# One ScalarE read of PSUM per quarter, differences and copies a slot later, extra banks and shorter routing in a two-layer expert and recurrence kernel

## What is computed

```python
x = x + 0.5 * ffn(layernorm(x))
x = x + attn(layernorm(x))
x = x + 0.5 * ffn(layernorm(x))

def ffn(x):                                   # 8 experts, 512 hidden channels, the best 2 of 8 count
    probs = softmax(x @ router_w.T)
    top_w, top_idx = top_k(probs, 2);  top_w = top_w / (sum(top_w) + 1e-9)
    y = relu(x @ w1[e].T + b1[e]) @ w2[e].T + b2[e]          # for every e
    return sum over the two chosen e of top_w * y
def attn(x):                                  # a gated linear recurrence over time, 4 heads, 16 keys, 32 values
    S = exp(w_t) * S + k_t v_t ;  o_t = q_t (S + u k_t v_t)
    o = groupnorm(o) * gn_weight + gn_bias;  return (o * silu(g)) @ W_o.T
```

## Time and profile before

| | |
|---|---|
| median of 3 runs | 491.46 us |
| the profiled execution's own time | 491.48 us |
| its span, first to last instruction | 489.6 us |
| TensorE busy | 477.3 us, 97% |
| VectorE busy | 367.5 us, 75% |
| ScalarE busy | 338.0 us, 69% |
| GpSimd busy | 240.8 us, 49% |
| TensorE's granted clock | 1.00 over the whole span |

### The profile page before, as it was taken

One profiled execution on the slowest core, in us unless ns is written; L12 is line 12 of the kernel. 1 busy time (PEld: TensorE's weight loads), 2 busy tenths in 40 slices (PEclk: granted clock), 3 DMA queues, 4 the chain that ended last, 5 costly groups with the idle time before them and its releaser, 6 DMA issues.

```text
span 489.6 us, 6291 instructions
## 1 busy us (share of the span) xinstructions
PE 477.3 (97%) x1873; PEld 302.0 (62%) x1873; DVE 367.5 (75%) x714; ACT 338.0 (69%) x569; POOL 240.8 (49%) x252
## 2 busy tenths in 40 slices
PE   8999999999999999999999999999999999999996
PEld 4676776566557556555755755565566565777775
DVE  3889877759975895997496799935669994667644
ACT  3776787677757668773857767646778765687874
POOL 3235632627875162886516268834616874321322
PEclk9999999999999999999999999999999999999999
DMA  7771121058410017730003555111046611003200
GB/s 252 233 269 33 54 64 41 7 154 234 129 43 1 1 44 208 204 106 1 1 2 129 150 175 151 44 64 43 1 120 182 195 43 44 0 1 117 79 1 21
DMA packets 21297, 44.59 MB, mean 91 GB/s; under 512 B 3856, under 2 KB 4240, under 8 KB 21264
## 3 DMA queue, kind: packets, MB, share of 16 engines
q1 hardware_dynamic: 14928, 32.66, 21.5%
q10 hardware_dynamic: 6336, 11.54, 8.3%
HBM read 40.91 MB, written 3.28 MB: 90 GB/s over the span
## 4 chain that ended last, share of the span: by engine, by line
PE 58%; issue 16%; POOL 11%; DVE 10%; ACT 3%; DMA 1%; POOLq 0%; ACTq 0%; DVEq 0%
PE Y L377 12%; PE U L346 8%; PE U L350 7%; PE U L347 7%; POOL qs L955 5%; PE Y L368 4%; PE Y L373 4%; PE Y L370 4%; POOL xT L929 4%; DVE hid_lo L773 2%; PE A L450 2%; PE A L442 1%; POOL pool_a L961 1%; PE A L436 1%; DVE gy L782 1%
## 5 line engine op out<-in xcount | busy, mean ns | idle before, releaser
L929 POOL TENSOR_TENSOR xT<-xT,gy 128x512 f32<-128x512 f32 x63 | 84.3, 1338 | 146.2 <-DVE gy L782 146.0
L346 PE MATMUL U<-xhi,w1lo 128*128 128x512 f32 x256 | 151.6, 592 | 3.0 <-ACT hid_hi L575 1.2
L377 PE MATMUL Y<-hid,w 128*128 128x512 f32 x264 | 134.2, 589 | 0.0
L773 DVE TENSOR_TENSOR hid_lo<-hid,hid_hi 128x512 fp32r<-128x512 f32 x124 | 97.8, 793 | 39.0 <-ACT hid_hi L575 38.5
L577 ACT ACTIVATE hid<-U,small 128x512 f32<-128x512 f32 x132 | 90.6, 689 | 48.6 <-PE U L350 46.2
L574 ACT ACTIVATE hid<-U,small 128x512 f32<-128x512 f32 x124 | 85.5, 690 | 43.8 <-PE U L350 39.3
L350 PE MATMUL U<-xlo,w1hi 128*128 128x512 f32 x256 | 100.8, 394 | 0.0
L347 PE MATMUL U<-xhi,w1hi 128*128 128x512 f32 x256 | 100.5, 392 | 0.0
L955 POOL TENSOR_TENSOR qs<-q,pool_a 128x512 f32<-128x512 f32 x64 | 80.1, 1251 | 15.0 <-DVE pool_a L830 14.8
L346 PEld LDWEIGHTS U<-xhi,w1lo 128*128 128x128 f32 x256 | 48.1, 188 | 62.1 <-issue 35.9
L575 ACT ACTIVATE hid_hi<-U,small 128x512 fp32r<-128x512 f32 x124 | 84.8, 684 | 0.0
(11 more groups left out here) (135 smaller groups left out, 515.9 us busy)
## 6 DMA issues: line engine op xcount, KB each, us to landing
G<-gate_dram SPq DMA_DIRECT2D x32, 512.0 KB, 4.3
vb<-v_dram ACTq DMA_DIRECT2D x44, 256.0 KB, 3.6
vb<-v_dram SPq DMA_DIRECT2D x20, 256.0 KB, 4.5
pool_a<-wexp_dram SPq DMA_DIRECT2D x8, 256.0 KB, 6.8
w<-wexp_dram SPq DMA_DIRECT2D x8, 256.0 KB, 6.8
v_dram<-v SPq DMA_DIRECT2D x8, 256.0 KB, 2.2
xnt<-xtok_dram SPq DMA_DIRECT2D x4, 256.0 KB, 5.1
xT<-xT_dram SPq DMA_DIRECT2D x4, 256.0 KB, 7.1
```

What stands on the lines that cost most here:

```text
L346: mm(dst, w1lo[:, e, f, :], xhi[:, k % NB, :], start=True, stop=False)
L377: last = mm(dst, w2[:, g % E, f, :], hid[:, n % HS, cut], start=first, stop=final)
L773: dve.tensor_tensor(hid_lo[:, c, :], hid[:, n % HS, :], hid_hi[:, c, :], ALU.subtract).then_inc(h_lo, 1)
L929: pool.tensor_tensor(xT[:, h, b, :], xT[:, h, b, :], gy[:, g % 2, :], ALU.add).then_inc(acc, 1)
```

## The change

1. ScalarE reads PSUM once a quarter. `h_f` is counted after that one instruction. The upper part is copied from `hid` in SBUF by a new `upper(n - 1)` that stands behind `relu(n)`, a slot later, with a semaphore of its own (`h_hi`).
2. VectorE's difference of quarter n is made in slot n+2 instead of n+1. TensorE still takes it in slot n+3.
3. Parts: quarters 112, 144 and 192 lose them, twelve fourth quarters (51, 83, 123, 167, 171, 215, 219, 235, 239, 243, 247, 251) gain them. For these VectorE makes the upper part too (a cast, then the difference), and all three down matmuls wait for it. In all 133 quarters in parts. `PS` goes from 3 to 4 buffers. GpSimd splits the fourth quarters of w2 in slots 33 to 41.
4. w1's upper parts of experts 2 to 7 are made on GpSimd, ahead of w2's, instead of on VectorE.
5. Experts 2 and 3 sum in banks A1 and A2, which are free in the first block, and the first two combines move to slots 13 and 14.
6. Routing works on the exponentials before they are normalised: 17 linked small instructions a block instead of 20, in 9 steps, which for block 1 are spread over 9 slots instead of 5.

```diff
+ROUTE = 9
-FP, PS, GS, VS = 3, 3, 6, 5
+FP, PS, GS, VS = 3, 4, 6, 5
+def route_slots(k):
+    return {1: 9, 2: 5, 3: 5}.get(k, 3)
 def route_steps(k, t):
+    return [1 + n for n in range(ROUTE) if n * route_slots(k) // ROUTE == t]
-    return 4 * g + {0: 10}.get(g, 7)
-LATE = (slot_of(2, T_PO) + 1, slot_of(2, T_PO) + 5)
+    return 4 * g + {0: 13, 1: 10}.get(g, 7)
+LATE = (112, 144, 164, 168, 192)
+LAST_PARTS = (33, 37, 39, 41)
+QUIET = (51, 83, 123, 167, 171, 215, 219, 235, 239, 243, 247, 251)
+def by_vector(n):
+    return n % FC == FP and n in QUIET
...
-    return n >= FC and n % FC < (1 if scans else FP) and n not in LATE
+    return n >= FC and n % FC < (1 if scans else FP) and n not in LATE or by_vector(n)
...
+        def rows_of(g):
+            return A[g - 1] if g in (2, 3) else Y[g % 2]
...
-                if f == 0 and g >= 2:
-                    pe.wait_ge(comb, g - 1)
+                if f == 0 and g >= 4:
+                    pe.wait_ge(comb, g - 1 if g >= 6 else g - 3)
...
+                    if not by_vector(n):
+                        pe.wait_ge(h_hi, uppers_to(n + 1))
+                    if f == FP:
+                        pe.wait_ge(w2lo_s, E + g % E // 2 + 1)
+                        pe.wait_ge(h_lo, parts_to(n + 1))
...
-                    act.activation(hid[:, n % HS, :], U[n % 2][:, :], ACT.Relu, bias=bias)
-                    act.activation(hid_hi[:, c % PS, :], U[n % 2][:, :], ACT.Relu, bias=bias).then_inc(h_f, 1)
+                act.activation(hid[:, n % HS, :], U[n % 2][:, :], ACT.Relu, bias=w(W_B1 + n % (E * FC), 1)).then_inc(h_f, 1)
+            def upper(n):
+                if n >= 0 and in_parts(n) and not by_vector(n):
...
+                    act.activation(hid_hi[:, c % PS, :], hid[:, n % HS, :], ACT.Copy).then_inc(h_hi, 1)
...
                 relu(n)
+                upper(n - 1)
...
-                    dve.wait_ge(h_f, n + 1)
+                    if not by_vector(n):
+                        dve.wait_ge(h_hi, uppers_to(n + 1))
+                    else:
+                        dve.wait_ge(h_f, n + 1)
+                        dve.wait_ge(down, PARTS[PARTS.index(n) - PS] + 1)
+                        link(dve.tensor_copy(hid_hi[:, c, :], hid[:, n % HS, :]))
...
-                if n >= 1:
-                    split_h(n - 1)
+                if n >= 2:
+                    split_h(n - 2)
...
+            def w1_upper(e):
+                pool.wait_ge(w1_in[e], 16)
+                if e == 2:
+                    pool.wait_ge(w1hi_s, 2)
+                pool.tensor_copy(w1hi[:, e].rearrange("p f n -> p (f n)"), w1raw[:, e, :]).then_inc(w1hi_s, 1)
...
+                if n % 4 == 0 and n // 4 + 2 < E:
+                    w1_upper(n // 4 + 2)
```

More of the change, by code:

```diff
@@ L117, in combine_slot, with uppers_to @@
 def combine_slot(g):
-    return 4 * g + {0: 10}.get(g, 7)
-LATE = (slot_of(2, T_PO) + 1, slot_of(2, T_PO) + 5)
+    return 4 * g + {0: 13, 1: 10}.get(g, 7)
[4 more added lines that the diff above has]
+    return n % FC == FP and n in QUIET
 def in_parts(n):
     scans = any(slot_of(i, T_SC) - 3 <= n < slot_of(i, T_PO if i == UNITS - 1 else T_OUT) for i in range(UNITS))
-    return n >= FC and n % FC < (1 if scans else FP) and n not in LATE
+    return n >= FC and n % FC < (1 if scans else FP) and n not in LATE or by_vector(n)
 def parts_to(n):
     return sum(in_parts(k) for k in range(n))
+def uppers_to(n):
+    return sum(in_parts(k) and not by_vector(k) for k in range(n))
 PARTS = [n for n in range(ALL) if in_parts(n)]
@@ L170, in program @@
         gate_T = sb("gate_T", [P, NB, 32])
-        w2hi = sb("w2hi", [P, E, FP, P], F32R)
-        w2lo = sb("w2lo", [P, E, FP, P], F32R)
+        w2hi = sb("w2hi", [P, E, FC, P], F32R)
+        w2lo = sb("w2lo", [P, E, FC, P], F32R)
         G = sb("G", [P, GS, NT])
@@ L220, in program @@
         half_s, hv_r, hr_r, hx_r, hr_p = (sem(n) for n in ("half_s", "hv_r", "hr_r", "hx_r", "hr_p"))
-        up, h_f, h_lo, down = sem("up"), sem("h_f"), sem("h_lo"), sem("down")
+        up, h_f, h_hi, h_lo, down = sem("up"), sem("h_f"), sem("h_hi"), sem("h_lo"), sem("down")
         w2hi_s, w2lo_s = sem("w2hi_s"), sem("w2lo_s")
@@ L738, in route @@
                 if step == 1:
+                    dve.wait_ge(lg_sub, k + 1)
+                    link(dve.scalar_tensor_tensor(out=flat(m(3)), in0=flat(m(0)), scalar=0.0, in1=flat(tie4),
+                                                  op0=ALU.is_equal, op1=ALU.mult))
+                    link(dve.tensor_reduce(r(5), m(3), AX.X, ALU.max))
+                if step == 2:
+                    link(dve.tensor_tensor(m(4), tie4, bc(r(5)), ALU.is_equal))
+                    link(dve.scalar_tensor_tensor(out=flat(m(6)), in0=flat(m(4)), scalar=-1e30, in1=flat(m(0)),
+                                                  op0=ALU.mult, op1=ALU.add))
@@ new lines, in route @@
+                if step == 3:
+                    link(dve.tensor_reduce(r(4), m(6), AX.X, ALU.max))
+                    link(dve.tensor_tensor(m(3), m(6), bc(r(4)), ALU.is_equal))
+                if step == 4:
+                    link(dve.tensor_tensor(m(3), m(3), tie4, ALU.mult))
+                    link(dve.tensor_reduce(r(5), m(3), AX.X, ALU.max))
+                if step == 5:
+                    link(dve.tensor_tensor(m(5), tie4, bc(r(5)), ALU.is_equal))
+                    link(dve.tensor_tensor(m(7), m(4), m(5), ALU.add))
@@ L749, in route @@
[L749 to L759 removed]
+                    link(dve.tensor_tensor(m(3), m(7), m(1), ALU.mult))
@@ L760, in route @@
+                if step == 7:
+                    link(dve.tensor_reduce(r(3), m(3), AX.X, ALU.add))
+                    link(dve.scalar_tensor_tensor(out=r(6), in0=r(1), scalar=1e-9, in1=r(3), op0=ALU.mult, op1=ALU.add))
+                if step == 8:
+                    link(dve.reciprocal(r(7), r(6)))
+                if step == 9:
+                    link(dve.scalar_tensor_tensor(out=gate[:, b].rearrange("p e t -> p t e"), in0=m(3), scalar=0.5, in1=bc(r(7)),
                                                   op0=ALU.mult, op1=ALU.mult))
-                if step == 5:
-                    link(dve.scalar_tensor_tensor(out=r(6), in0=r(3), scalar=1e-9, in1=r(4), op0=ALU.add, op1=ALU.add))
-                    link(dve.reciprocal(r(7), r(6)))
-                    link(dve.tensor_tensor(gate[:, b].rearrange("p e t -> p t e"), m(3), bc(r(7)), ALU.mult))
@@ L781, in combine @@
                     dve.wait_ge(acc, g - 1)
-                dve.scalar_tensor_tensor(out=gy[:, g % 2, :], in0=Y[g % 2][:, :], scalar=w(W_B2 + e, 1),
+                dve.scalar_tensor_tensor(out=gy[:, g % 2, :], in0=rows_of(g)[:, :], scalar=w(W_B2 + e, 1),
                                          in1=G[:, g % GS, :], op0=ALU.add, op1=ALU.mult).then_inc(comb, 1)
@@ L915, in _ @@
                     attend(i, step_of(i, n))
+            split_h(ALL - 2)
             split_h(ALL - 1)
@@ L1075 @@
     arrays = lay_out(inputs)
-    nc = bacc.Bacc("TRN2", target_bir_lowering=False, num_devices=1)
+    nc = bacc.Bacc("TRN2", target_bir_lowering=False, num_devices=1, dynamic_dma_scratch_size=1024)
     args = [nc.dram_tensor(n, a.shape, F32, kind="ExternalInput").ap() for n, a in arrays.items()]
```

48 lines of the change are left out of this document (16 added, 32 removed).

## The result

The changed kernel takes **502.1 us** (median of 4 runs, 501.08 to 502.86), the kernel before 491.38 beside it: a ratio of 1.0218, 95% interval 1.0206 to 1.0231. Forecast was 486.4, range 482.8 to 489.6. It is 2.2% slower and outside the range. The profiled execution took 501.08 us, 9.6 more than the one of before, so 14.7 us over the forecast's sum.

A forecast was written before the change was run, and what follows sets the result against it. The prediction took TensorE to bound the kernel, with 10.5 us of small gaps. Its terms summed to -5.05 us, taking 491.48 to 486.4 us, range 482.8 to 489.6.

The forecast's parts named there:

- What bounds the kernel: Whole kernel: TensorE follows its instructions nearly everywhere, with 10.5 us of small gaps left over.
- In steady slots the difference ended 2.6 us before its matmul, so 1.39 later is free.: Differences a slot later: no cost in steady slots; +0.9 us in preparation of the units, bounds 0 and 3.
- rise from 0.2 us to 2 or 3: Sign to look for: TensorE's total wait for hid_lo, at quarters 42, 46, 88, 104, 174 and 230.
- Free: Items put at no cost: TensorE's waits at h_hi, w2 splits in slots 33 to 41, the fourth buffer.
- First block, -3.0: First block: casts leave VectorE and routing spreads, closing gaps of 3.2 us; -3.0 us, bounds 0 and -3.2.
- Quarters in parts, -1.4: Twelve quarters gained, three lost, at 0.155 us of TensorE each: -1.4 us if nothing waits.
- Rival C: The twelve casts meet GpSimd and each holds TensorE 0.2 us beyond the slack: +2.4, 488.8 us; chance 0.12.
- ScalarE frees the bank, slots 38 to 41, +0.3: Bank free 0.57 us sooner, but VectorE late next: between 1.5 us gained and 1.5 lost, taken as +0.3.
- Scans: Four scans: units 0 to 3 at +0.2, -0.5, -1.8 and -0.95 us; bounds together -4.4 and +1.
- Last block's gate rows, +0.9: Quarter 230's difference queues behind the combine waiting for the gate rows' DMA: +0.9 us, bounds 0.3 and 1.6.
- The end, +0.3: Quarter 254's copy stands behind quarter 255's relu, its difference ending at 484.8 against a matmul at 484.52: +0.3 us.
- Rival B: TensorE's third down matmul waits for differences stuck behind VectorE work: 493.4 us, deciding above 4.4 us of waits; chance 0.06.

The follow-up runs named there:

- run 6: The changed kernel with ScalarE's two PSUM reads in one slot as before, the difference still in slot n+2: 497.78 us, ratio 1.0120.
- run 10: The kernel of run 2 with the twelve fourth quarters taken out of parts: 491.51 us, ratio 1.0006.
- run 2: The changed kernel with ScalarE's two PSUM reads in one slot and the difference back in slot n+1: 489.09 us, ratio 0.9959.
- run 11: The kernel of run 2 with the first block's combines back in the slots of the kernel before: 487.6 us, ratio 0.9924.
- run 9: The kernel before with only the single PSUM read, late upper copy and difference in slot n+2 added: 506.6 us, ratio 1.0304.
- run 3: The changed kernel without the twelve fourth quarters in parts: 502.16 us, ratio 1.0219.
- run 7: The changed kernel with all down matmuls a slot later (n+4), six hid buffers and combines at 4g+8: 490.36 us, ratio 0.9977.
- run 4: The changed kernel with w1's upper casts of experts 2 to 7 back on VectorE: 502.55 us, ratio 1.0220.

## Why the prediction was wrong

**What bounds the kernel** was right: TensorE, broken by short waits. That hid_lo would be the new wait was right as well, and so were several places: 42, 46, 88, 104, 140, 174, 230 and the end. The sizes and the number of places were not: the other seven places make 6.9 of the 11.7 us.

**The step that failed: "In steady slots the difference ended 2.6 us before its matmul, so 1.39 later is free."** A steady slot has room, but 15 differences do not stand in one, and the sum's list of those that don't was short. I costed 42, 88, 104, 174, 140, 181, 230 and the end, some 3 us in all ("rise from 0.2 us to 2 or 3"), and TensorE waited 11.7. Quarters 13, 14 and 18, 41, 130, 148 and 215 were not in the list or called in time; 46 stands among the signs but not in the sum. Run 6 makes this step alone cost 8.4 to 8.7 us. Two errors lie in it. I checked a moved difference against the row in whose place it lands, one quarter at a time, without running VectorE's whole order forward with it; and I gave each 0.69 us, although the spread of rows 6 (1783 ns at most) was in front of me and I used it for the casts only. For quarter 174 I added 0.69 although its row in rows 11 says 0.86.

**A second term was put at nothing: the late copy.** Under *Free* I asked whether TensorE would wait at `h_hi`, and it does not. But VectorE's difference waits for the same copy, and that I did not price. From run 6 to the change it costs 4.3 to 4.6 us: a wait of 0.22 us for the copy puts a difference behind the start of an addition instead of ahead of it (run 10), and the last one too; how it costs the 1.3 us of slots 40 to 48 is not shown.

**First block, -3.0, measured +1.4.** The gaps that I wanted to close were closed (no wait for w1's remainder), and three waits for hid_lo of 3.33 us came in their place. Even with two reads and the early difference (run 2) this block was 1.1 us behind; the shifted combines take 2.0 us of it (run 11). Without them (run 11) slot 24 is 0.9 us ahead of the kernel before, but 0.4 of that is there at slot 0, before any part of the change works (run 9, without these parts, has 0.35 there); so the gain is some 0.5, a sixth of what I took.

**Quarters in parts, -1.4.** The size was right: run 10 gives 2.4 us for the twelve by the medians and 1.8 by the profiles, where 12 x 0.155 is 1.9. Rival C did not happen. No cast was slow; source L800 of the kernel after (least, median, most ns):

```profile
L800 DVE CAST hid_hi<-hid x12: 414/417/429, 108.6 to 488.1; 128x512 fp32r<-128x512 f32 x12
```

But C's "against", that the addition has ended two slots before the cast, was wrong too: in slots 243 to 245 it ended at 475.98 and the cast began at 476.45. The difference ahead of the cast met the addition, and the cast inherited its delay (runs 3 and 10).

**ScalarE frees the bank, slots 38 to 41, +0.3.** Waits for the second read are gone. Quarters 41, 42 and 46 took 2.0 us instead. Rows have the copy at 623 ns against 688 for the relu: as costed.

**Scans: over their slots (56 to 120, 136 to 208) the forecast has -2.2 in all, measured +0.3.** Signs were right for units 2 and 3; the third scan began 5.45 us later than before, in a slot that TensorE entered 6.46 later, so 1.0 us sooner in its place. The scans' own gaps went, and quarters 104, 140 and 148 gave back 1.7.

**Last block's gate rows, +0.9.** Quarter 230 waited 0.38 us, the mechanism was as told: VectorE's wait for the gate rows was 1.82 us, 1.0 shorter than before. **The end, +0.3**: 1.4, since the difference of 254 took 1.67 us beside the last but one addition, not 0.69; without the late copy (run 6) the end is as before.

**Rival B** was the right one in its mechanism: "the difference becomes the bound", deciding above 4.4 us of new waits. It had 0.06 and a price of 493.4, 8.7 under the measured time, from a list that had 46 and 130 but nothing of the first block. Its waits were 6.0, the measured ones 11.7.

What stays open: how the 6.0 us that are neither a waiting difference's own slowness nor the slot alone divide between the slot and slow instructions further ahead. No run here takes the collisions away while the difference stays late, so the division of the loss between queue and collision rests on readings of the trace, while that the two together with the missing slot make it is shown (runs 2, 6, 7 and 9).

## What to carry to other kernels

An operation may be deferred by a slot only if every instance of it still makes its deadline with its slow duration, not its median, and with whatever stands ahead of it in its engine's order; look first at the instances that stand in slots full of other work. Where VectorE works on two SBUF operands beside GpSimd's additions, put the two next to each other in a known order: a difference begun before the addition took 0.68 us (and the addition 1.68 for 1.29), one begun behind it 1.69. And try the parts of a change in pairs: here four of six gained 0.4% (0.8% with the combines left where they were), and the other two cost 2.7% and hid it.

## What the runs showed of the hardware

That an idle stretch of TensorE of only 2 us is followed by half the clock in some executions and not in others I had not expected. Runs of the change lie in two groups, 501.08 and 501.38, 502.82 and 502.86. The profiled one, at full clock throughout, is of the first. Five profiles have this wait, of 1.98 or 1.99 us; the clock falls behind it in three (runs 3, 4 and 9) and not in two (the change and run 6). In the profile of run 3 (502.81 us) it falls as in run 9:

```profile
268.00:270.00 2.00, 1.20 (x5) 0.77 0.37 72
270.00:272.00 2.00, 2.00 (x6) 0.50 0.00 0
```

A wait of that length therefore costs 2.0 us or 3.6. That the upper group of the change has the fall as well is inferred from its times and not seen in a trace. The mean clocks do not settle it: they are 0.996 and 0.997 there, but 0.997 for the execution of 501.38 too.
